# Two chunks of products moved ahead of the seam between two programs, and two row splits moved up on VectorE

## The reference

```python
h = _L0_tok_ref(x, L0_tok_h0)                       # filter, twice: 750 -> 192 steps
h = h + _L0_attn_ref(_layernorm(h), Wk, Wr, Wo, time_decay, time_first)
# experts, on xn = _layernorm(h), with gates from the two best router logits:
hid = jax.nn.relu(jnp.einsum('bsd,df->bsf', xn, w1) + bb1)
y = jnp.einsum('bsf,fd->bsd', hid, w2) + bb2
acc = acc + y * c[..., None]
```

## Time and profile before

| | |
|---|---|
| median of 3 runs | 962.48 us (961.36 to 963.33) |
| profiled execution, its time | 958.76 us |
| its span | 957.0 us |
| TensorE busy | 910.1 us |
| VectorE busy | 778.4 us |
| ScalarE busy | 614.0 us |
| GpSimd busy | 547.2 us |

### The profile page before, as it was taken

How to read it: one execution, slowest core, us unless ns; L and a number is a source line. 1 busy time by engine, 2 the same in 40 slices (tenths; PEclk the granted TensorE clock), 3 DMA queues, 4 the chain that set the end, 5 groups by cost and what they waited for, 6 DMA issues and landing times. The chain is left out here.

```text
span 957.0 us, 17357 instructions
## 1 busy us (share of the span) xinstructions
PE 910.1 (95%) x5838; PEld 778.1 (81%) x5838; DVE 778.4 (81%) x2020; ACT 614.0 (64%) x1182; POOL 547.2 (57%) x463
## 2 busy tenths in 40 slices
PE   5899999999877999999999999999999999999996
PEld 4567666676655899999989999999999999999995
DVE  2799999999997877777877877787787787879774
ACT  2899999999973455555655655555465564556552
POOL 1003464657886666656755656774665665567543
PEclk9999999999998999999999999999999999999998
DMA  8664445363241355556565546655556655555732
GB/s 264 230 230 145 158 135 169 113 236 118 66 159 55 126 142 155 146 143 191 110 192 142 145 139 186 182 133 152 139 147 202 165 146 145 129 156 147 216 45 34
DMA packets 73297, 144.33 MB, mean 151 GB/s; under 512 B 9069, under 2 KB 62430, under 8 KB 69242
## 3 DMA queue, kind: packets, MB, share of 16 engines
q0 software_dynamic: 31136, 99.92, 38.6%
q1 hardware_dynamic: 42074, 43.30, 13.9%
HBM read 111.36 MB, written 31.83 MB: 150 GB/s over the span
## 5 line engine op out<-in xcount | busy, mean ns | idle before, releaser
L1886 ACT ACTIVATE kpad<-kr_ps,b 128x512 f32<-128x512 f32 (+1 forms) x240 | 152.9, 637 | 236.6 <-PE kr_ps L1944 236.4
L1840 POOL DMA_INDIRECT out_rows<-yout,dest x108 | 182.3, 1688 | 42.3 <-issue 33.0
L2219 DVE CAST hhi<-kpad 128x512 fp32r<-128x512 f32 (+1 forms) x240 | 104.9, 437 | 103.5 <-ACT kpad L1886 102.7
L1944 PE MATMUL kr_ps<-xhi,whi 128*128 128x512 f32 (+1 forms) x488 | 182.4, 374 | 5.0 <-issue 2.1
L1944 PE MATMUL kr_ps<-xlo,whi 128*128 128x512 f32 (+1 forms) x488 | 179.3, 367 | 0.0
L1944 PE MATMUL kr_ps<-xhi,wlo 128*128 128x512 f32 (+1 forms) x488 | 178.6, 366 | 0.0
L1866 ACT ACTIVATE whi<-h 128x512 fp32r<-128x512 f32 x240 | 147.5, 623 | 32.1 <-DMA h<-in_ew,idx 29.7
L1990 DVE TENSOR_TENSOR wlo<-h,whi 128x512 fp32r<-128x512 f32 x240 | 162.6, 684 | 3.1 <-ACT whi L1866 3.0
L2221 DVE TENSOR_TENSOR hlo<-kpad,hhi 128x512 fp32r<-128x512 f32 (+1 forms) x240 | 152.3, 635 | 8.2
L196 POOL DMA_INDIRECT h<-token_rows,tile_tid x110 | 117.1, 1064 | 61.0 <-issue 60.8
L181 POOL DMA_INDIRECT expert_lists<-tokens,slots x96 | 126.6, 1319 | 26.8 <-issue 25.3
(11 more groups left out here) (247 smaller groups left out, 1904.7 us busy)
## 6 DMA issues: line engine op xcount, KB each, us to landing
frames<-in_x SPq DMA_DIRECT2D x32, 512.0 KB
frames<-in_x SPq DMA_DIRECT2D x32, 256.0 KB
token_rows<-xs SPq DMA_DIRECT2D x16, 388.5 KB, 4.9
out_rows<-h SPq DMA_DIRECT2D x16, 384.0 KB, 2.6
expert_lists<-setup SPq DMA_DIRECT2D x12, 280.0 KB
h<-token_rows,tile_tid POOLq DMA_INDIRECT x110, 3.6
out_rows<-yout,dest POOLq DMA_INDIRECT x110, 3.9
expert_lists<-tokens,slots POOLq DMA_INDIRECT x96, 2.8
```

Source lines behind the costliest of these rows:

```text
L1840: pool.indirect_dma_start(out[:, :], bass.IndirectOffsetOnAxis(dest[:, j.i, r:r + 1], 0), yout[:, j.s, r, :], None, compute_op=ALU.add).th ...
L1886: act.activation(hid[:, c % 2, 0:j.r * P], hp[c % 2][:, 0:j.r * P], ACT.Relu, bias=b1[:, j.s, c:c + 1]).then_inc(hid_done, 1)
L1944: last = pe.matmul(hp[c % 2][:, 0:j.r * P], w_[j.s][:, at:at + P], x_[j.s][:, k, 0:j.r * P], start=n == 0, stop=n == 3 * HC - 1)
L2219: dve.tensor_copy(hhi[:, c % 4, 0:j.r * P], hid[:, c % 2, 0:j.r * P]).then_inc(hhi_done, 1)
```

## The change

Two edits. On TensorE, `first_up(4)` and `first_up(5)` are added to the end of the first program, after `first_down(1)`, and the second program leaves these two out, while `down`, the transposes and everything else keep their order: its first products are now `down(T0, 2)`. On VectorE, `x_low(T1, 0)` stands before the step `tiles_each()` instead of after it, and `x_low(T1, 1)` directly after that step, instead of after `experts_of_tiles()`.

```diff
-EARLY, EARLY_PIECES = 4, 5
+EARLY, EARLY_UP, EARLY_PIECES = 4, 6, 5
...
                 ranks(pair[15])
                 first_down(1)
+                first_up(4)
+                first_up(5)
...
                 for c in range(EARLY if j.first() else 0, FC):
-                    up(j, c)
+                    if not j.first() or c >= EARLY_UP:
+                        up(j, c)
                     if c >= 2:
                         down(j, c - 2)
...
                 low(6)
+                x_low(T1, 0)
                 tiles_each()
-                x_low(T1, 0)
+                x_low(T1, 1)
                 ends_of_big()
                 w_low(T1, 3)
                 ends_of_half()
...
                 past_half()
                 low(7)
                 experts_of_tiles()
-                x_low(T1, 1)
                 one_hot()
```

## The result

| | before | changed |
|---|---|---|
| median of 20 runs | 961.96 us | 957.95 us |
| lowest to highest | 959.99 to 966.78 | 953.90 to 965.30 |
| profiled execution | 958.76 us | 954.22 us |
| its span | 957.0 us | 952.4 us |
| granted clock over that span | 0.989 | 0.990 |

The ratio is 0.9955, 95% interval 0.9939 to 0.9971: the changed kernel is faster, by 2.8 to 5.9 us. The forecast was 2.8 us less (959.7), and the direction was right. Set against the interval, its size is at the small end.

The account below looks back on a forecast made before the run. TensorE's nearly unbroken product chain was taken as the bound, with gaps of 1.8 and 2.1 us near the seam. `down(T1, 0)` moving from 330.68 to 327.9 gives 962.48 - 2.8 = 959.7 us; own range 958.7 to 960.6, wide 957.9 to 961.8.

Parts of the forecast that it names:

- second row split ready, at the latest: On VectorE before tile 1: `x_low(T1, 1)` done by 319.5 us, ahead of TensorE's coming at 320.1.
- wait of TensorE there: At `down(T1, 0)`: TensorE is there at 327.2 us but waits 0.7 us for VectorE's first low half of tile 1.
- GpSimd free ahead of the list row of tile 3: GpSimd, starting its second program 1.45 us later, is free at 330.6 us instead of 329.1.
- gain at the seam: Start of `down(T1, 0)`, first down of tile 1, moves from 330.68 to 327.9 us: 2.8 us less.
- TensorE's first event at the seam: At L224, where all engines meet between the two programs: TensorE's comes last, near 310.35 us, the release 0.1 later.
- The 1.1 us wait of TensorE stays what it is: TensorE's later wait on ScalarE, after the seam, was taken as unchanged by the change.
- The rule on the clock: TensorE's clock rise differs from run to run, so the moved products ahead of the seam may run slow in other runs.
- The transfer takes the gain: Tile 3's weights, not issued earlier, stop TensorE in tile 2: gain only 2.1 us, or 0.7; chance 0.13.
- VectorE keeps pace: At `down(T1, 0)` TensorE does not wait for VectorE: gain 3.5 us (959.0); chance 0.62 together with the forecast.
- Loading the second program's code: At the seam, code fetch stands bare: gain 1.4 us, chance 0.15 shared with the late clock; longer stall, slower, 0.05.
- The clock rises later: Moved products ahead of the seam run at half clock: gain 1.4 us (961.1); chance 0.15 shared with small code-loading stall.
- The gap moves whole to VectorE: Around the seam, VectorE keeps its old times, 1.45 us late: gain 0.25 us (962.2); chance 0.05.

Follow-up runs that it names:

- e3: Changed kernel with VectorE's two row splits put back, so only the two product groups moved ahead of the seam: median 961.26 us, ratio 0.9983 to the kernel before.
- e4: Changed kernel with chunks 4 and 5 put back behind the seam, so only the row splits moved: median 959.39 us, ratio 0.9991 to the kernel before.
- e2: The changed kernel, unedited, a second set of executions on the first chip: median 958.32 us, ratio 0.9964 to the kernel before.
- e12: The changed kernel, unedited, a third trace, run on the third chip: median 962.24 us, ratio 0.9967 to the kernel before.
- e1: The kernel before, unedited, run against itself on the first chip: median 961.35 us, ratio 0.9986.
- e9: Changed kernel with VectorE's last seven table steps moved behind the low half of tile 1's second chunk; third chip: median 964.76 us, ratio 0.9981 to before.
- e10: Changed kernel with GpSimd issuing tile 3's bias rows ahead of its weights instead of behind; third chip: median 967.70 us, ratio 0.9996 to the kernel before.
- e6: Changed kernel with VectorE's last seven table steps moved behind tile 1's first low half; second chip: median 968.39 us, ratio 0.9957 to the kernel before.
- e8: Changed kernel with GpSimd issuing tile 3's bias rows ahead of its weights instead of behind; second chip: median 973.67 us, ratio 0.9975 to the kernel before.
- e7: Changed kernel with `first_down(2)` also moved ahead of the seam; second chip: median 972.67 us, ratio 0.9985 to the kernel before.

## Why the prediction was right at the seam and small for the whole

| step of the prediction | forecast | measured |
|---|---|---|
| last moved product ends | 310.28 | 310.22 |
| TensorE's arrival; the release | 310.35; 310.45 | 310.3; 310.6 |
| TensorE; VectorE restart | 310.75; 310.71 | 310.82; 310.77 |
| second row split ready, at the latest | 319.5 | 319.42 |
| low half ends; `down(T1, 0)` starts | 327.8; 327.9 | 327.88; 327.94 |
| wait of TensorE there | 0.7 | 0.60 |
| GpSimd free ahead of the list row of tile 3 | 330.6 | 331.68 |
| tile 3's weights issued | 1.1 earlier (341.4) | 341.53 |
| ScalarE's wait for weights ends | near 351 | 350.75 |
| gain at the seam | 2.8 | 2.7 (e3 1.2 and e4 1.6 alone; forecast 1.0 and 1.7) |
| median of before | 962.48 (3 runs) | 961.96 (20 runs) |
| difference of the medians | 2.8 | 4.0 in the first comparison, 3.7 in e2's, 4.0 in e12's (by the ratios 4.3, 3.5 and 3.2) |

**What held.** The three arguments that carried it were: TensorE had 1.3 us of slack ahead of SyncE; VectorE's waits at the seam were for relus whose products now end before it; and VectorE, not TensorE, would decide `down(T1, 0)`. Each is seen in the trace after and in the parts alone. One sign came out otherwise than written: TensorE's first event at the seam was to come after all others, and GpSimd's came 0.1 later still.

**What failed: the last step, from the seam to the whole.** The prediction took the 2.8 us of the seam off the median of three runs, 962.48, and came to 959.7, with 958.7 to 960.6 as its own range. The measured 957.95 is 1.7 below. Of this, 0.5 is the base: the median of before is 961.96 in 20 runs. The term that was mis-sized is the difference outside the seam, which the sum put at 0 and which measured 1.2 between the medians (4.0 less 2.8). The only reason given for the 0 was that "The 1.1 us wait of TensorE stays what it is", from the one trace of before. It did not stay: it is absent after, and absent in e1 with the code of before.

The runs show in its place that the time hangs on the granted clock of each execution: in the 20 runs of the changed kernel the clock lay between 0.979 and 0.993 and the time between 965.3 and 953.9. That is a spread of 11 us, and the prediction allowed 1 us either way for the median. In e2's comparison the clocks drawn account for 1.4 of 3.7, and at equal clock the change is worth 2.65 +- 0.89, with the forecast's 2.8 inside. For the first comparison the clocks of the runs of before are not on record. Had they been those of the 35 runs of before on the first chip (0.9854, median 962.06, against 961.96), the mean clock of 0.9869 in the changed kernel's 20 runs would account for 1.2 (an estimate, 1.5 times 0.82). So it is argued and not shown that the 1.2 has this source.

**The rule on the clock.** The Trainium skill ("TensorE: Matmul & The Clock Gate", What's actually happening) says that the point of the clock's rise differs from run to run. The traces agree: with the same code the granted clock ahead of the seam was 0.50 (1.2 GHz) until about 305.4 us in the changed kernel's first trace and until about 309.2 in e2, and 1.00 (2.4 GHz) from there on. From 262 to 300 us it was 0.94 in the one and 0.87 in the other, and SyncE came to the seam 3 us later in e2. The prediction used the rule only for a loss on the moved products. None was seen: the twelve ran at full clock in the trace after (2.89 from 307.33 to 310.22, forecast 2.91), and in all nine traces that have both groups ahead of the seam their first and last starts lie 2.50 to 2.54 apart. What the scatter did was to blur the sum by more than the change is worth.

**The rivals.** *The transfer takes the gain*: not in the traces of this change, but the cover is thin, as e9 and e10 show. *VectorE keeps pace*: no, TensorE waited 0.60; removing the backlog is worth 0.9 at `down(T1, 0)` (e6 and e9 18.3, against 19.2 in e8 and e12 on the same chips). *Loading the second program's code*: from TensorE's arrival to the release 0.3, then 0.2 to its first product, together 0.1 more than the forecast. TensorE's gap there was 0.57 to 0.63 in all ten traces in which it came last, so no load stood bare. *The clock rises later*: not in the traces after. *The gap moves whole to VectorE*: no, TensorE's wait at `down(T1, 0)` is 0.60, where the gap ahead of tile 1 was 2.06.

## What to carry to other kernels

Before work is moved across a meeting of all engines, ask who arrives last: here products placed ahead of it cost nothing until that arrival, and each microsecond beyond it held every other engine as long. A list of work on a busy second engine is judged by when its first consumer comes, so put what feeds the critical engine ahead of tables that nobody waits for yet. And a gain of 3 us is read from distances inside the trace, from one event to another, which repeated to 0.2 us here for the same code, and not from medians alone, since the granted clock moved them by several times that.

## What the runs showed of the hardware that I had not expected

- In 20 runs of one kernel the mean granted clock of an execution went with 86% of the scatter of its time (correlation -0.93, -0.76 us for each +0.001). In the other sets of runs the correlation was -0.57 to -0.97.
- One and the same kernel took 962.1, 972.9 and 966.2 us on three chips. On the two slower ones TensorE waited for relus far more often, here from 345 us to the end in e6 (second chip) and e12 (third), where the changed kernel's first trace and e2 have no row for a relu:

```profile
PE kr_ps L1946 <- ACT kpad L1888: 6.2, 6, 1.3
PE kr_ps L1946 <- issue: 1.3, 2, 1.1
```

```profile
PE kr_ps L1946 <- ACT kpad L1888: 2.8, 2, 1.5
PE kr_ps L1946 <- issue: 2.6, 2, 2.4
```

- Only some of these relus stood behind a weight transfer: two of the six in e6 (at 816.70 and 901.33) and one of the two in e12 (at 492.28). Shortly ahead of four of the other five ScalarE had idled 3.6 to 3.7 us, put down to "remote". What that is stays open.
- A stop that the profile puts down to "issue" can be a plain wait for another engine. The longest one in e12 ended 0.10 after VectorE's second row split, which that product needs, and those of 2.19 in e8, 2.42 in e10 and 1.13 in e7 ended 0.10 to 0.11 after theirs. So did the gap of 2.06 that this change removed (0.11). ScalarE, VectorE and TensorE in e12:

```profile
395.51 0.69 ACT L1888 ACTIVATE kpad<-kr_ps,b 128x512 f32<-128x512 f32 x1 [4.04 <-PE kr_ps L1946]
396.23 0.43 DVE L2222 CAST hhi<-kpad 128x512 fp32r<-128x512 f32 x1 [3.38 <-ACT kpad L1888]
...
397.91 0.68 DVE L1997 TENSOR_TENSOR xlo<-cnt_ps,xhi 128x512 fp32r<-128x512 f32 x1
398.69 0.47 PE L1946 MATMUL kr_ps<-xhi,whi 128*128 128x512 f32 x1 [2.35 <-issue]
```

- The split was late because VectorE had waited 3.38 for a relu, and that relu started 3.4 after the last of its products had ended (392.09). None of these runs tells what held ScalarE there; it stays open.
